# Two products with 64 weight columns in place of one with 128, in the search for each node's last edge

## The chip, the cores and the metric

The kernel runs on one core of a Trainium2 chip. The metric is the device time of one execution in microseconds, measured without the profiler. The program is one launch: two layers of a graph network (a normalisation, a graph convolution, an attention and a feed-forward part each) over 6250 nodes and 100000 edges, 256 features per node, float32.

## The reference

Only the first part of each layer matters here. The second layer's convolution takes for every node the features of the last edge that names it; which edge that is does not depend on the features, so the kernel finds it early, while the first layer's convolution runs.

```python
def _L0_gnn_ref(x, W, edge_index):
    src, dst = (edge_index[0], edge_index[1])
    h = x @ W
    deg = jax.ops.segment_sum(jnp.ones_like(dst, dtype=h.dtype), dst, num_segments=N)
    deg_inv_sqrt = jnp.where(deg > 0, jax.lax.rsqrt(jnp.maximum(deg, 1)), 0.0)
    norm = deg_inv_sqrt[src] * deg_inv_sqrt[dst]
    msgs = h[src] * norm[:, None]
    out = jax.ops.segment_sum(msgs, dst, num_segments=N)
    return out

def _L1_gnn_ref(x, edge_index, W, b):
    dst, src = (edge_index[0], edge_index[1])
    agg = jnp.zeros_like(x).at[dst].set(x[src])     # the last edge wins
    h = jnp.concatenate((x, agg), axis=-1)
    return h @ W.T + b

edge_index = jnp.stack([src, dst])
xn = _layernorm(x, axis=-1)
x = x + _L0_gnn_ref(xn, L0_gnn_W, edge_index) + _L0_mix_ref(...)[0]
x = x + _L0_ffn_ref(...)[0]
xn = _layernorm(x, axis=-1)
x = x + _L1_gnn_ref(xn, edge_index, L1_gnn_W, L1_gnn_b) + _L1_mix_ref(...)[0]
x = x + _L1_ffn_ref(...)[0]
```

## The kernel before

The program is a row of stages. The change touches one of them, `gather_stage` (names that begin with `gcn_` in the profile), which does the first layer's convolution, most of its attention, and the search for last edges.

The edges lie sorted by target in 784 tiles of 128 (padded). Four tiles make a group (GE = 4), so there are G = 196 groups, and two groups make a pair (PT = 8 tiles, 98 pairs). Per group POOL (GpSimd) issues four indirect gathers (L945; 782 in all, as the last group is short) that fetch 128 rows of `h_table` each into one of eight buffers `msg`; DVE builds one-hot matrices `hot` from the targets (`targets`, L1028); TensorE sums the messages by target, `acc = hot.T @ msg`, four float32 products of 128x128 weights and 256 columns (`sum_up`, L1152; each float32 product runs as two, so the profile has eight per group); DVE adds the sums to X (`add_up`, L1037).

Per pair the kernel also looks for the last edges. A source number is split into a low part (0 to 127) and a high part (0 to 48). DVE makes `lo_hot` (128 lanes, 128 low parts, 8 tiles, bf16, L1020) and `hi_eq` (49 high parts, L1023); ACT multiplies the latter with a power of two that grows with the lane, which gives `hi_hot` (`place`, L874). For each of the 8 tiles TensorE makes one product, `see` (L1159): weights `lo_hot[:, :, c]`, 128 rows and 128 columns, and moving operand `hi_hot[:, :, c]`, 49 columns. The tile is the last index of both, so two neighbouring columns of either operand lie 8 bf16 numbers (16 bytes) apart. The eight results lie side by side in one PSUM bank `seen`; the exponent of a sum names the highest lane, which is the last edge of the tile. ACT copies the bank (`keep_seen`, L879), and DVE merges the copy into what was seen so far by two predicated copies (`last_edges`, L1045 and L1047).

The order on each engine is written out by hand: the engines run through loops over eight groups, and the semaphores couple them. TensorE's queue for a pair is: sum of the even group, sum of the odd group, `see`, with the attention's products between (keys and values in the first loop, L1179 to L1184; the attention's output in the second, L1190 and L1191; nothing in the third). DVE's queue per group is: one-hots for the group four ahead (`sources`, `targets`), `add_up`, `last_edges`. So a merge that waits for `see` holds back the one-hots of the next group. POOL may run four groups ahead of TensorE: before group g it waits until group g-4 is summed (`after(pool, summed, g - NG + 1)`, NG = 4).

Two other products are of use for comparison. In the stage ahead `count_in` (L644, `front_deg`) makes products of 64 weight columns, bf16, with 98 moving columns; its operands' neighbouring columns lie 2 numbers (4 bytes) apart. In the last stage L2796 (`sel_ranks`) has 128 weight columns and 50 moving columns, bf16, also 4 bytes apart.

Of the kernel before, what the change touches and what calls it, by code (L numbers as in the profile page):

```python
# [24 lines left out]
P = 128  # L25
# [3 lines left out]
T = -(-N_NODES // P)  # L29
# [29 lines left out]
def after(eng, sem, n):  # L59

    if isinstance(n, int) and n <= 0:
        return
    eng.wait_ge(sem, n)
# [184 lines left out]
class Kernel:  # L248
# [456 lines left out]
    def gather_stage(self):  # L705

        nc, io = self.nc, self.io
# [5 lines left out]
        NS = 4  # L713
        NP = 2
# [3 lines left out]
        with ExitStack() as ctx:  # L718
# [3 lines left out]
            lo_hot = [s.sb(f"lo_hot{i}", [P, P, PT], BF16) for i in range(NS // 2)]  # L722
            hi_eq = [s.sb(f"hi_eq{i}", [P, T, PT], BF16) for i in range(2)]
            hi_hot = [s.sb(f"hi_hot{i}", [P, T, PT], BF16) for i in range(NS // 2)]
# [60 lines left out]
            seen = s.banks("seen", NP, PT * T)  # L785
# [66 lines left out]
            with nc.Block() as block:  # L852
# [287 lines left out]
                def _(pe):  # L1140
# [14 lines left out]
                    def see(h, k):  # L1155
                        after(pe, hi_ready, h + 1)
                        after(pe, lasts_kept, 2 * (h - NP + 1))
                        for c in range(PT):
                            last = nc.tensor.matmul(seen[k % NP][:, c * T:(c + 1) * T], lo_hot[k % NS][:, :, c], hi_hot[k % NS][:, :, c], start=True, stop=True)  # L1159
                        last.then_inc(seen_ready, 1)  # L1160

                    def groups(q, n):
                        for b in range(n):
                            sum_up(NB * q + b, b, q)
                            if b % 2 == 1:
                                see(NB // 2 * q + b // 2, b // 2)
# [26 lines left out]
                    for g in range(CHUNKED * NB):  # L1193
                        b, q = g % NB, g // NB
                        sum_up(g, b, q)
                        if b % 2 == 1:
                            see(g // 2, b // 2)
                        if g < NC:
                            key_chunk(g)
# [5 lines left out]
                    with pe.Fori(CHUNKED, ATT) as q:  # L1205
                        for b in range(NB):
                            n = NK * (q - CHUNKED) + sum(x < b for x in SLOTS) + 2
                            if b in SLOTS:
                                keys_and_values(n, SLOTS.index(b) % 2, P)
                            sum_up(NB * q + b, b, q)  # L1210
                            if b % 2 == 1:
                                see(NB // 2 * q + b // 2, b // 2)
                            if b in SLOTS:
                                context(n, P)
# [5 lines left out]
                    for b in range(KB):  # L1220
                        last = nc.tensor.matmul(side[:, b * D:(b + 1) * D], qc[:, b * P:(b + 1) * P], w_out, start=True, stop=True)
# [1693 lines left out]
```

## Time and profile before

| | us |
|---|---|
| median of three runs | 2759.92 (2756.18 to 2763.06) |
| span of the profiled execution | 2735.8 |
| median less span: what lies around it | 24.1 |
| gather stage, first gather issued to last one ended | 137.9 to 1280.2 |
| TensorE busy over the whole span | 2240.2 (82%) |
| POOL busy over the whole span | 1616.4 (59%) |
| DVE busy over the whole span | 1457.9 (53%) |
| the products of L1159, 784 of them, in the page's groups by form | 47.8 + 44.6 |

The span is the time from the first to the last instruction of one profiled execution. The profile gives no total for that execution beside its span; the median of the unprofiled runs is 24.1 us (0.9%) longer, which is launch and completion around it. The columns "busy" are sums over instructions; PE is TensorE's matmul side, PEld its weight loads. In a timeline, several instructions of one kind that follow each other are merged to one row with their count.

### The profile page before, as it was taken

How to read it: one execution, taken by the hardware profiler on the slowest of the kernel's cores; microseconds unless marked ns; L12 is line 12 of the kernel's file. 1: busy time of each engine (PE TensorE's matmuls, PEld its weight loads, DVE VectorE, ACT ScalarE, POOL GpSimd, SP SyncE). 2: the span in 40 equal slices, each digit the busy share in tenths (PEclk: the TensorE clock that was granted, in tenths of full speed). 3: DMA queues.
4: the chain of work that ended last, by engine and by line, in shares of the span. 5: the costliest groups of instructions: out<-in, count | busy, mean ns of one | idle time of the engine just before them, and what ended most of it. 6: DMA issues, size and time to landing. Idle time of an engine off the chain costs nothing. (4 is left out here: it accounts for less than half of the span.)

```text
span 2735.8 us, 47046 instructions
## 1 busy us (share of the span) xinstructions
PE 2240.2 (82%) x12461; PEld 1829.5 (67%) x12462; DVE 1457.9 (53%) x4032; ACT 826.7 (30%) x2317; POOL 1616.4 (59%) x2089
## 2 busy tenths in 40 slices
PE   7876767767666766655889999989998999996898
PEld 5644555555554544444869999967767888885798
DVE  9754433434444454435842223259987777777211
ACT  2511221221111111111623333335553333332333
POOL 5676666666666666764036555447857666661232
PEclk9987787878877886676589999999999999997999
DMA  4233332322333333333323334323221111111121
GB/s 159 98 99 87 88 92 86 90 86 86 91 90 87 91 91 92 92 90 85 118 77 106 106 123 138 104 78 101 88 68 55 44 46 42 44 46 62 30 37 29
DMA packets 139022, 227.27 MB, mean 83 GB/s; under 512 B 26923, under 2 KB 99456, under 8 KB 138946
## 3 DMA queue, kind: packets, MB, share of 16 engines
q0 software_dynamic: 56240, 142.70, 18.8%
q1 hardware_dynamic: 81186, 82.10, 9.0%
q10 hardware_dynamic: 1520, 1.58, 0.2%
q8 instruction: 34, 0.56, 0.1%
q14 instruction: 42, 0.34, 0.0%
HBM read 174.97 MB, written 51.30 MB: 83 GB/s over the span
## 5 line engine op out<-in xcount | busy, mean ns | idle before, releaser
L945 POOL DMA_INDIRECT all_XN<-h_table,l_srcI x782 | 780.3, 998 | 367.3 <-issue 219.1
L1152 PE MATMUL gcn_acc<-all_XN,gcn_hot 128*128 128x256 f32 x796 | 257.6, 475 | 110.9 <-DVE all_X L1037 54.4
L1152 PE MATMUL gcn_acc<-all_XN 128*128 128x256 f32 x768 | 248.1, 478 | 110.9 <-DVE all_X L1037 59.5
L1152 PEld LDWEIGHTS gcn_acc<-all_XN,gcn_hot 128*128 128x128 f32 x796 | 179.1, 236 | 171.6 <-DVE all_X L1037 76.6
L1152 PEld LDWEIGHTS gcn_acc<-all_XN 128*128 128x128 f32 x768 | 175.2, 239 | 164.6 <-DVE all_X L1037 69.5
L879 ACT COPY gcn_seen_sb<-gcn_seen 128x392 f32<-128x392 f32 x98 | 47.6, 485 | 576.2 <-remote 454.8
L1848 ACT ACTIVATE moe_hidden<-moe_hid_ps,moe_b 128x128 f32<-128x128 f32 x420 | 131.5, 364 | 281.5 <-PE moe_hid_ps L1929 250.0
L1929 PEld LDWEIGHTS moe_hid_ps<-moe_xst,held_held 128*128 128x128 f32 x1680 | 204.2, 193 | 12.0 <-issue 7.4
L1037 DVE SCALAR_TENSOR_TENSOR all_X<-gcn_acc,all_XN,all_X 128x256 f32 x392 | 170.6, 475 | 74.7 <-remote 59.2
L1929 PE MATMUL moe_hid_ps<-moe_xst,held_held 128*128 128x128 f32 x1680 | 207.5, 277 | 1.9 <-DVE moe_xst L1869 1.9
L1045 DVE COPY_PREDICATED gcn_last_seen<-gcn_seen_sb,gcn_seen 128x392 f32<-128x392 int32 x98 | 57.7, 589 | 277.6 <-ACT gcn_seen_sb L879 190.1
L1936 PE MATMUL moe_y_ps<-held_held,moe_hidden 128*128 128x256 f32 x840 | 198.9, 380 | 0.0
L2539 PE MATMUL att_f_ps<-held_held 128*128 128x256 f32 x784 | 191.0, 388 | 7.5 <-ACT held_held L2406 7.5
L2529 PE MATMUL att_hid_ps<-att_xpt,held_held 128*128 128x128 f32 x1568 | 184.2, 276 | 0.0
L2529 PEld LDWEIGHTS att_hid_ps<-att_xpt,held_held 128*128 128x128 f32 x1568 | 180.3, 193 | 0.1
L2539 PEld LDWEIGHTS att_f_ps<-held_held 128*128 128x128 f32 x784 | 141.7, 190 | 43.5 <-ACT held_held L2406 23.5
L1936 PEld LDWEIGHTS moe_y_ps<-held_held,moe_hidden 128*128 128x128 f32 x840 | 151.0, 190 | 16.9 <-issue 0.2
L1763 POOL DMA_INDIRECT moe_ring<-rows_table,moe_row x108 | 105.9, 981 | 84.0 <-POOL moe_row L1761 68.1
L1869 DVE COPY moe_xst<-moe_turned 128x256 f32<-128x256 f32 x106 | 45.0, 425 | 151.7 <-PE moe_turned L1909 125.8
L2060 POOL DMA_INDIRECT held_held<-slots_out,all_slot x98 | 99.6, 1016 | 36.0 <-issue 23.4
L1184 PE MATMUL gcn_tab<-all_XN 128*128 128x129 f32 (+1 forms) x98 | 27.2, 367 | 112.2 <-ACT all_XN L891 75.7
L2406 ACT ACTIVATE held_held<-att_hid_ps,early_b 128x128 f32<-128x128 f32 x392 | 111.4, 368 | 17.6 <-PE att_hid_ps L2529 17.6
(433 smaller groups left out, 4596.7 us busy)
## 6 DMA issues: line engine op xcount, KB each, us to landing
held_held<-in_e_w SPq DMA_DIRECT2D x32, 512.0 KB
slots_out<-moe_y SPq DMA_DIRECT2D x105, 128.0 KB
all_XN<-h_table,l_srcI POOLq DMA_INDIRECT x782
all_X<-in_x SPq DMA_DIRECT2D x7, 896.0 KB, 11.2
rows_table<-all_XN SPq DMA_DIRECT2D x7, 896.0 KB, 4.2
z_table<-held_held SPq DMA_DIRECT2D x49, 128.0 KB
x_table<-all_XN SPq DMA_DIRECT2D x49, 128.0 KB, 1.7
out<-all_X SPq DMA_DIRECT2D x49, 128.0 KB, 1.7
```

Source lines behind the costliest of these rows:

```text
L945: nc.gpsimd.indirect_dma_start(msg[b][:, c, :], None, self.h_table, bass.IndirectOffsetOnAxis(self.srcI[:, GE * g + c:GE * g + c + 1], 0)) ...
L1037: nc.vector.scalar_tensor_tensor(x, acc[b % NA][:, :], scale[:, k, ds(g, 1)], x, ALU.mult, ALU.add).then_inc(added, 1)
L1045: nc.vector.copy_predicated(last_seen[:, :], seen_sb[k % 2][:, :], seen[k % NP][:, :]).then_inc(lasts_kept, 1)
L1152: last = nc.tensor.matmul(acc[b % NA][:, :], hot[b % NH][:, c, :], msg[b][:, c, :], start=(c == 0), stop=(c == n - 1))
L1763: nc.gpsimd.indirect_dma_start(ring[:, k * D:k * D + D], None, self.rows_table, bass.IndirectOffsetOnAxis(row_1[k][:, :], 0)).then_inc(lan ...
L1848: last = nc.scalar.activation(hidden[:, 2 * k + f, :], hid_ps[k][:, f, :], ACT.Relu, bias=b1[:, c:c + 1])
L1929: last = nc.tensor.matmul(hid_ps[k][:, f, :], w1[p][:, q, c:c + P], xst[:, q, :], start=(q == 0), stop=(q == KB - 1))
L1936: last = nc.tensor.matmul(y_ps[:, :], hidden[:, f, :], w2[p][:, f, :], start=(f == 0), stop=(f == FB0 - 1))
L2060: nc.gpsimd.indirect_dma_start(ys[t % 2][:, c, :], None, self.slots_out, bass.IndirectOffsetOnAxis(self.slot[:, t, c:c + 1], 0)).then_inc( ...
L2406: last = nc.scalar.activation(hidden[:, c, :], hid_ps[k][:, f, :], ACT.Relu, bias=b1[:, c:c + 1])
L2529: last = nc.tensor.matmul(hid_ps[k][:, f, :], W1[:, b, c:c + P], xpt[:, b, :], start=(b == 0), stop=(b == KB - 1))
L2539: last = nc.tensor.matmul(f_ps[:, :], hidden[:, f, :], W2[:, f, :], start=(f == 0), stop=(f == FB1 - 1))
```

## The change

Each product of `see` becomes two. The first has the weight columns 0 to 63 and writes the lanes 0 to 63 of `seen`; the second has the columns 64 to 127 and writes the lanes 64 to 127. Both stream the same 49 moving columns. The 64 is the number of weight columns; all 128 rows are still used, and what is computed is the same. The semaphore is still raised by the last product alone. Per pair there are 16 products and 16 weight loads where there were 8 and 8; over the program 784 more of each.

```diff
@@ -1156,7 +1156,8 @@
                         after(pe, hi_ready, h + 1)
                         after(pe, lasts_kept, 2 * (h - NP + 1))
                         for c in range(PT):
-                            last = nc.tensor.matmul(seen[k % NP][:, c * T:(c + 1) * T], lo_hot[k % NS][:, :, c], hi_hot[k % NS][:, :, c], start=True, stop=True)
+                            for half in (slice(0, P // 2), slice(P // 2, P)):
+                                last = nc.tensor.matmul(seen[k % NP][half, c * T:(c + 1) * T], lo_hot[k % NS][:, half, c], hi_hot[k % NS][:, :, c], start=True, stop=True)
                         last.then_inc(seen_ready, 1)
```

On TensorE, in the body of the second loop (with the attention's output), the queue before reads as follows; the numbers behind a name are left out, x8 counts products, and L63 is the code of a wait.

```order
240 L1152 MATMUL gcn_acc<-all_XN,gcn_hot 128x256 x4
241 L63 ISA x2
242 L1159 MATMUL gcn_seen<-gcn_hi_hot,gcn_lo_hot 128x49 x8
243 L63 REGISTER_ALU x2
244 L1190 MATMUL gcn_side<-l_M,all_XN 128x256 x2
245 L1191 MATMUL gcn_side<-l_W,all_ones 128x256
```

And of the kernel with the change, in the same place (its lines behind L1159 are one higher):

```order
240 L1152 MATMUL gcn_acc<-all_XN,gcn_hot 128x256 x4
241 L63 ISA x2
242 L1160 MATMUL gcn_seen<-gcn_hi_hot,gcn_lo_hot 64x49 x16
243 L63 REGISTER_ALU x2
244 L1191 MATMUL gcn_side<-l_M,all_XN 128x256 x2
245 L1192 MATMUL gcn_side<-l_W,all_ones 128x256
```

Nothing has moved; the eight products with 128 output lanes have become sixteen with 64, between the same neighbours. The other engines' instructions are the same.

## Rows read from the trace of the kernel before

**Rows 1.** Windows of the whole gather stage, of its first loop and of its third
```profile
core 0: us, PE busy (x) PEld busy (x) DVE busy (x) ACT busy (x) POOL busy (x), PEclk, DMA share, GB/s
137.90:1280.20 1142.30, 774.37 (x3078) 573.02 (x3079) 504.38 (x1070) 206.44 (x488) 780.28 (x782) 0.78 0.31 90
400.00:500.00 100.00, 73.64 (x311) 57.57 (x312) 38.83 (x80) 21.79 (x63) 66.20 (x67) 0.78 0.30 88
1100.00:1200.00 100.00, 61.75 (x210) 43.46 (x211) 43.86 (x92) 15.28 (x30) 70.50 (x70) 0.71 0.32 92
```

**Rows 2.** Waits in the stage: who waited for whom, us in total, times, longest
```profile
ACT gcn_seen_sb L879 <- remote: 454.8, 55, 25.9
DVE gcn_last_seen L1045 <- ACT gcn_seen_sb L879: 190.1, 29, 21.3
...
POOL all_XN L945 <- remote: 107.5, 45, 4.1
ACT gcn_seen_sb L879 <- PE gcn_seen L1159: 98.9, 27, 7.2
...
POOL all_XN L945 <- PE gcn_acc L1152: 34.5, 19, 7.5
```

**Rows 3.** Timeline near 440 us (idle before, releaser); last a window as in rows 1
```profile
437.58 1.99 PE L1152 MATMUL gcn_acc<-all_XN,gcn_hot 128*128 128x256 f32 x8
...
439.20 0.91 PEld L1159 LDWEIGHTS gcn_seen<-gcn_hi_hot,gcn_lo_hot 128*128 128x128 bf16 x8
...
439.41 0.92 PE L1159 MATMUL gcn_seen<-gcn_hi_hot,gcn_lo_hot 128*128 128x49 bf16 x8
440.48 0.94 POOL L945 DMA_INDIRECT all_XN<-h_table,l_srcI  x1 [0.30 <-issue]
...
444.23 0.80 PE L1184 MATMUL gcn_tab<-all_XN 128*128 128x129 f32 x2 [3.90 <-ACT all_XN L891]
...
447.50 0.49 ACT L879 COPY gcn_seen_sb<-gcn_seen 128x392 f32<-128x392 f32 x1 [2.80 <-remote]
447.56 0.94 POOL L945 DMA_INDIRECT all_XN<-h_table,l_srcI  x1 [2.38 <-remote]
...
439.20:440.40 1.20, 1.13 (x10) 0.84 (x8) 0.00 (x0) 0.00 (x0) 0.95 (x1) 1.00 0.36 109
```

**Rows 4.** Durations of L1159: ns min/median/max, first and last start, form
```profile
L1159 PEld LDWEIGHTS gcn_seen<-gcn_hi_hot,gcn_lo_hot x400: 140/146/175, 157.1 to 1276.6; 128*128 128x128 bf16 x134
L1159 PE MATMUL gcn_seen<-gcn_hi_hot,gcn_lo_hot x400: 246/274/287, 157.3 to 1276.7; 128*128 128x49 bf16 x134
```

**Rows 5.** Timeline near 1047 us, where the same products stand apart
```profile
1046.03 0.15 PEld L1159 LDWEIGHTS gcn_seen<-gcn_hi_hot,gcn_lo_hot 128*128 128x128 bf16 x1 [1.58 <-issue]
1047.43 0.14 PEld L1159 LDWEIGHTS gcn_seen<-gcn_hi_hot,gcn_lo_hot 128*128 128x128 bf16 x1 [1.26 <-issue]
...
1046.73 0.25 PE L1159 MATMUL gcn_seen<-gcn_hi_hot,gcn_lo_hot 128*128 128x49 bf16 x1 [1.86 <-issue]
1048.13 0.25 PE L1159 MATMUL gcn_seen<-gcn_hi_hot,gcn_lo_hot 128*128 128x49 bf16 x1 [1.15 <-issue]
```

**Rows 6.** L2796, one burst of ten; its window (busy, granted clock); its durations
```profile
2534.87 0.57 PE L2796 MATMUL sel_ranks<-sel_node_part,all_XT 128*128 128x50 bf16 x10 [6.17 <-ACT sel_node_part L2659]
...
2534.80:2540.40 5.60, 2.80 (x50) 0.50 0.00 0
...
L2796 PEld LDWEIGHTS sel_ranks<-sel_node_part,all_XT x49: 102/119/123, 2534.8 to 2540.2; 128*128 128x128 bf16 x49
L2796 PE MATMUL sel_ranks<-sel_node_part,all_XT x49: 200/217/220, 2534.9 to 2540.2; 128*128 128x50 bf16 x49
```

**Rows 7.** Durations of L644 (64 weight columns) and of its neighbour L667
```profile
L644 PEld LDWEIGHTS front_deg<-all_XN x784: 107/109/172, 8.3 to 101.5; 128*64 128x64 bf16 x196
L644 PE MATMUL front_deg<-all_XN x784: 205/208/290, 8.3 to 101.6; 128*64 128x98 bf16 x196
...
L667 PE MATMUL front_h_ps<-l_W,all_XT x196: 379/379/763, 45.5 to 132.3; 128*128 128x256 f32 x196
```

**Rows 8.** Timeline near 61 us, around sixteen products of L644; last its window
```profile
60.13 0.69 DVE L560 TENSOR_TENSOR all_XN<-front_dst_lo,all_XN 128x1024 bf16<-128x1024 bf16 x1
60.18 1.03 PE L667 MATMUL front_h_ps<-l_W,all_XT 128*128 128x256 f32 x4
...
61.14 0.78 PEld L644 LDWEIGHTS front_deg<-all_XN 128*64 128x64 bf16 x16 [0.33 <-DVE all_XN L560]
61.14 0.92 PE L644 MATMUL front_deg<-all_XN 128*64 128x98 bf16 x16
...
61.99 0.44 PE L653 MATMUL front_turned<-all_ident,all_XN 128*128 128x128 f32 x2
...
61.10:62.10 1.00, 1.00 (x18) 0.89 (x18) 1.00 (x2) 0.69 (x2) 0.96 (x2) 1.00 0.00 0
```

**Rows 9.** Timeline near 905 us: `see` behind a slow sum, then a fast one
```profile
901.96 3.41 PE L1152 MATMUL gcn_acc<-all_XN 128*128 128x256 f32 x8 [3.27 <-DVE all_X L1037]
...
905.20 0.92 PE L1159 MATMUL gcn_seen<-all_XN 128*128 128x49 bf16 x8
...
905.94 1.93 PE L1152 MATMUL gcn_acc<-all_XN,gcn_hot 128*128 128x256 f32 x8
```

## The prediction

> **What bounds the kernel now.** I read the busy shares first, then cut out the stage that holds `see`, then its waits, and last the timeline. The stage takes 1142 of 2736 us, and nobody is full in it: TensorE is busy 774 us (68%), POOL 780 (68%), DVE 504 [rows 1]. The pace is POOL's. A gather takes 0.94 us and the next follows 0.30 later [rows 3], so a group of four takes 4.96 us and the 782 gathers 782 x 1.24 = 970 us. The remaining 172 us of the stage are gathers that came late. POOL waited 107.5 us in 45 waits that the profile calls remote and 34.5 us in 19 waits for the sum L1152 [rows 2]: 64 waits, 142 us, in which the sum four groups back was not yet reported. So TensorE's time costs something where its queue is late, and nothing else.
>
> How late it can be is seen near 440 us: the sum ended at 439.57 (437.58 + 1.99) and `see` at 440.33, but POOL went on at 447.56 and ACT copied `seen` at 447.50 [rows 3]. Between them TensorE had nothing of them to do. I don't know what holds these reports back; it is a part of the 142 us that is not TensorE's work, and I keep it apart. ACT's and DVE's large waits, 454.8 and 190.1 us, are of this kind, with 98.9 us that ACT waits for `see` itself [rows 2].
>
> **The change part by part.** Removed: 8 products and 8 loads per pair. Added: 16 and 16. No engine but TensorE has other work. A `see` now takes 0.92 us [rows 3, 9]. Its last product lasts 0.27 [rows 4], so the products start (0.92 - 0.27)/7 = 93 ns apart.
>
> What are the 93 ns? L2796 has the same shape, 128 weight columns and 50 moving ones, and its ten products take 0.57 us, (0.57 - 0.22)/9 = 39 ns apart, at half clock (0.50, that is 1.2 GHz) [rows 6]. In L1159 the pace is 93 ns at full clock (1.00, 2.4 GHz) [rows 3]. The difference between the two in the code is the distance of neighbouring columns, 16 bytes against 4. And it shows on the moving side: where the loads of L1159 stand 0.70 us ahead of their products, with the weights long in place, a product still takes 0.25 us [rows 5], while a product with twice the columns, 98, takes 0.208 [rows 7] and one with 50 columns 0.217 at half clock [rows 6]. If 98 columns close together cost 98/2.4 = 41 ns (L644 ran at 1.00 [rows 8]), the fixed part is 0.167 and the 49 distant ones cost some 80 ns, nearly the whole pace. The halved products stream the same 49 columns. So I take 93 ns for each half, and 15 x 0.093 + 0.27 = 1.67 us for the sixteen: **+0.75 us** per `see`.
>
> The bounds of this pace: below, L644 with its 64 weight columns makes sixteen products in 0.92 us [rows 8], (0.92 - 0.21)/15 = 47 ns apart, which gives 15 x 0.047 + 0.25 = 0.96 us, +0.04. Below that, with L2796's 39 ns or less, and if two halves ran side by side at some 25 ns apiece, 15 x 0.025 + 0.25 = 0.63, -0.29. Above, if 64 weight columns are read one by one as slowly as the moving ones (93/49 = 1.9 ns a column), a load lasts 122 ns and is the pace: 15 x 0.122 + 0.27 = 2.10, +1.18. I stay at 93, the measured pace of the same operands.
>
> The second term is the passage between the two shapes. L667's last product starts at 60.18 + 1.03 - 0.38 = 60.83; at its pace of 0.216 ((1.03 - 0.38)/3) the next would start at 61.05, and L644 starts at 61.14: 0.09 late. The DVE instruction named there had ended at 60.82 [rows 8], so it was not that. Leaving: L644's last product starts at 61.14 + 0.92 - 0.21 = 61.85, 0.047 later would be 61.90, and L653 starts at 61.99: 0.09 late. In `see` before there is no such loss on leaving: last start 905.20 + 0.92 - 0.27 = 905.85, next product 905.94, one pace of 0.09 [rows 9]. So **+0.18 us** per `see`; the bounds are 0 and 0.2. The Trainium skill, "TensorEngine Tiling (Array Packing)", section "Tiling Modes", says that changing the tiling mode drains the TensorE, while changing the tile within a mode does not; the trace agrees with the first (0.09 us each way), and by the second the change between lower and upper half adds nothing, which I assume too.
>
> Together 0.75 + 0.18 = 0.93 us per `see`, 98 x 0.93 = 91 us more TensorE work in a stage where TensorE is idle 1142 - 774 = 368 us. What lands? In steady pace nothing: in the third loop TensorE has 61.75 us of work in 100 us [rows 1], about 7.1 us for a pair (100/70 x 8 = 11.4 us for its eight gathers, times 0.62) against the 9.9 us that POOL needs; 8.0 still fits. In the first loop (73.6 in 100, a pair per 11.9 us) 8.8 becomes 9.7: just. What hides the addition is thus POOL's pace, and it is gone where POOL waits. The sum that POOL waits for has, in TensorE's queue and since the last free moment, about one `see` ahead of it (there is one for two sums). The 19 waits for L1152 grow by 0.93 us each in full; of the 45 remote ones I count two thirds, 30, since part of them ends on the unexplained delay and not on work. 49 x 0.93 = **+45 us**. There is a second path of the same length: ACT's copy comes 0.93 later, DVE's merge behind it, and behind the merge in DVE's queue the one-hots for a later sum [rows 2]; it runs into the same waits of POOL and is not counted twice.
>
> Against its own execution: 2735.8 + 45 = 2781 for the span, and 24.1 around it gives 2805, which is the median 2759.9 + 45. No difference under 0.3% (8 us) can be told from none here.
>
> **The rivals.**
> (a) The weight load becomes the pace: 0.122 us a product, 1.18 + 0.18 = 1.36 us per `see`, 49 x 1.36 = 67 us, 2827. For it: L1159's loads last 146 ns against 119 in L2796 at half clock [rows 4, 6], so they too are slowed by the distance. Against: L644's loads with 64 columns last 109 [rows 7], less than those of 128. By the Trainium skill, "TensorE: Matmul & The Clock Gate", section "Weight-path perf modes", the fast weight load applies only to 128 weights that are not fp32, and the tiling page's list of incompatibilities has column tiling exclude it; the halves would then lose it. That is the mechanism under which 0.122 would hold, and no row of before has 64 columns at this distance.
> (b) Everything is hidden: the waits end on the delayed reports alone, as at 447.56 [rows 3], and POOL's pace covers the rest. Then 0 to 8 us, about 2763. For it: TensorE itself had been idle for 3.90 us when it went on at 444.23 [rows 3], so its queue was not the cause there. Against: 19 waits are put down to L1152.
> (c) Faster: the two halves have different weights and different output lanes and run side by side, so that `see` takes 0.63 + 0.18 = 0.81 us or less, and with no loss at the passages 0.63. Price: 64 x -0.29 = -19 us, 2741. It decides from a pace below 44 ns per product (15 x 0.044 + 0.25 = 0.92). For it: 25 to 39 ns is possible for this engine [rows 6]; against: the moving columns' 80 ns, and the passages. The Trainium skill, "TensorE: Matmul & The Clock Gate", section "Part 3: Packing small matmuls", has small products on different column groups run concurrently; no row of before shows two such products together.
> (d) The late reports become more with the number of products (784 more on 3078 in the stage, +25%): the 142 us of waiting grow by a quarter, 36 us, on top of 45: about 2841.
>
> **How the numbers follow.** Forecast 2805: chance 0.45. (a) 0.17, (b) 0.18, (c) 0.13, (d) 0.07. Range: the low end leaves out most of (c), 2750; the high end takes in (a) and (d) together with all 64 waits at 1.36 + 36 us, 2760 + 87 + 36 = 2883, 2885. The likeliest case alone: 49 waits give 45, 19 waits 18 and all 64 with 0.93 60, so 2778 to 2820. Faster by over 0.3%: (c), 0.13, and 0.01 of (b). Within 0.3%: 0.15 of (b) and 0.03 of the forecast's lower edge, 0.18. Slower: the rest of the forecast 0.42, (a) 0.17, (d) 0.07 and 0.02 of (b), 0.68.
>
> **What would show it.** In the profile of the changed kernel a run of sixteen products should last 1.6 to 1.7 us (0.96 would be the lower bound, 2.1 rival (a), 0.6 to 0.8 rival (c)); a product alone still 0.25. The loads should be at or below 146 ns; 190 would be (a). The first product behind a sum should start 0.31 after the sum's last instead of 0.22. TensorE's work in the stage should be up by about 80 us and the granted clock by a few hundredths. The stage should be longer by 45 us, all in POOL's waits; gathers keep 0.94 + 0.30. Other stages should keep their times. I would be wrong if the run of sixteen is below 0.92 us, or if it is 1.6 us and the stage no longer.

## The result, and the profile after

| | before | after |
|---|---|---|
| median of six runs | 2758.05 us (2746.84 to 2763.06) | 2775.75 us (2771.28 to 2786.76) |
| ratio | | 1.0074, 95% interval 1.005 to 1.0097 |
| span of the profiled execution | 2735.8 us | 2776.9 us |

The change costs 18 to 20 us where 45 were forecast (2805). The direction and the range are right, the size is not. The two spans differ by 41 us. That is no measure of the change: the run in which the after profile was taken needed 2778.77 us, so only 1.9 us lie around a span. The profile of before came from an execution quicker than each of its timed runs. I had read the 24.1 us between its span and the median as launch and completion; most of it is scatter from one execution to the next.

Each of the 18 kernels below is compared only with runs of before from its own session, as before itself differs between sessions: its medians are 2743.17 us beside kernels 1 to 4, 2756.72 beside 5 to 8, 2756.79 beside 9 to 12, 2758.48 beside 13 to 16, and 2607.61 (23 runs, 2604.02 to 2612.08) beside 17 and 18. Kernels 5 to 8 and 17 and 18 ran on the same chip, so the 150 us are not a difference between two chips.

Windows of the kernel after, as in [rows 1] (columns as there):

```profile
137.90:1280.20 1142.30, 826.66 (x3733) 588.94 (x3734) 485.66 (x1030) 201.72 (x478) 750.24 (x755) 0.78 0.30 87
400.00:500.00 100.00, 77.60 (x363) 57.83 (x364) 43.37 (x89) 22.99 (x68) 64.64 (x65) 0.81 0.29 84
1100.00:1200.00 100.00, 59.99 (x262) 43.80 (x263) 38.39 (x80) 13.91 (x27) 67.66 (x69) 0.69 0.31 90
```

TensorE has 52 us more busy time in the same 1142 us, and POOL has got through 755 gathers instead of 782. Before and after, cut where the stage of each ends:

```profile
130.00:1290.00 1160.00, 782.07 (x3112) 578.86 (x3110) 512.24 (x1089) 209.97 (x496) 781.42 (x784) 0.78 0.31 90
1290.00:2735.00 1445.00, 1351.46 (x8280) 1165.13 (x8280) 830.71 (x2699) 562.64 (x1694) 756.76 (x1148) 0.94 0.25 74
```

```profile
130.00:1330.00 1200.00, 858.20 (x3894) 611.77 (x3892) 513.07 (x1089) 210.20 (x496) 780.31 (x784) 0.78 0.30 87
1330.00:2776.00 1446.00, 1351.41 (x8280) 1165.55 (x8280) 830.38 (x2698) 562.68 (x1694) 757.52 (x1148) 0.94 0.25 74
```

Behind the stage nothing has changed (1351.46 and 1351.41 us of TensorE work, 1445 and 1446 us). Inside it the instructions of the other engines are the same in number and cost, TensorE has 782 products more and 76 us more of busy time (41 of them in `see` itself, 92 to 133 us; the rest is spread over its other products).

`see` in the timeline of after near 441 us, against [rows 3, 9]:

```profile
437.86 3.26 PE L1152 MATMUL gcn_acc<-all_XN 128*128 128x256 f32 x8
439.99 0.95 POOL L945 DMA_INDIRECT all_XN<-h_table,l_srcI  x1 [1.49 <-remote]
...
441.05 1.18 PE L1160 MATMUL gcn_seen<-all_XN 128*64 128x49 bf16 x16
...
442.15 1.13 PE L1180 MATMUL gcn_side<-l_W,all_XN 128*128 128x256 f32 x4
...
449.88 1.16 PE L1160 MATMUL gcn_seen<-gcn_hi_hot,gcn_lo_hot 128*64 128x49 bf16 x13
451.49 0.36 PE L1160 MATMUL gcn_seen<-gcn_hi_hot,gcn_lo_hot 128*64 128x49 bf16 x3 [0.45 <-issue]
...
437.80:441.00 3.20, 3.20 (x10) 2.38 (x8) 0.88 (x2) 0.00 (x1) 1.65 (x2) 0.56 0.29 82
```

The sixteen products take 1.18 us where 1.67 were forecast. The sum at 437.86 takes 3.26 us instead of 1.99 [rows 3], but that is the clock and not the change: the granted clock around it is 0.56 (last line), and before has such sums too, 3.41 us at 901.96 [rows 9]. Something else is to be seen. The run of sixteen at 449.88 is broken once: the last three stand 0.45 us apart from the others with "issue" as the reason, so TensorE waited for nothing that the profile shows. By single records, such steps are 0.70 us from one instruction to the next, in bursts. I count in the stage the steps of 0.6 us or more, start to start, between two loads or products that stand next to each other in TensorE's records with no wait or other sequencer instruction at or between them: 50 before, with 40 us in them, and 143 after, with 115 us. I call them stalls. (The 62 and the "119 to 164" that an expectation below names come from a wider count of the same steps.) Half of them in after, 73, stand in the third loop.

The durations of the half products, against [rows 4]:

```profile
L1160 PEld LDWEIGHTS gcn_seen<-gcn_hi_hot,gcn_lo_hot x800: 192/217/226, 157.2 to 1317.7; 128*64 128x64 bf16 x160
L1160 PE MATMUL gcn_seen<-gcn_hi_hot,gcn_lo_hot x800: 246/300/348, 157.2 to 1317.8; 128*64 128x49 bf16 x160
```

The waits of after, against [rows 2]; the last line is one of before that is not shown there:

```profile
ACT gcn_seen_sb L879 <- remote: 515.7, 56, 22.8
...
POOL all_XN L945 <- remote: 128.1, 66, 4.0
ACT gcn_seen_sb L879 <- PE gcn_seen L1160: 122.9, 32, 7.3
PEld gcn_seen L1160 <- issue: 107.8, 165, 2.6
...
POOL all_XN L945 <- PE gcn_acc L1152: 64.4, 26, 15.3
...
PEld gcn_seen L1159 <- issue: 30.4, 45, 6.6
```

POOL's waits have grown from 142.0 to 192.5 us, by somewhat more than the 40 us between the two stages; as these are two single executions, and before's was a quick one, only about half of that can be the change. TensorE's own row is larger: 107.8 us of "issue" ahead of the loads of `see`, where before has 30.4.

The late reports themselves can be measured, as the trace also holds the time of each semaphore update. I set each update that reports a sum beside the last sum that had ended by then (20 of 193 updates of before are missing in the trace, and a lag longer than the distance of two sums is taken too short). In before the update comes 2.0 us after the sum's end in the median, 3.3 in the mean, and 110 of 173 come over 1 us late. Nearly all updates by DVE and ACT in this stage come 7 to 12 ns after their instructions' ends. So of these three engines TensorE alone reports late. In after they are no later: median 2.4 us, mean 3.1, 119 of 185 over 1 us.

### The profile page after: what moved, and what is told of

Same layout as the page of the kernel before. It is cut to its first block and busy times, and to the rows that moved or that the text cites. A ratio compares the mean times of both kernels' runs of the same rounds, so it can differ in the third digit from the quotient of the medians.

```text
span 2776.9 us, 48614 instructions
## 1 busy us (share of the span) xinstructions
PE 2317.1 (83%) x13245; PEld 1863.4 (67%) x13246; DVE 1458.3 (53%) x4032; ACT 827.2 (30%) x2317; POOL 1616.1 (58%) x2089
## 5 line engine op out<-in xcount | busy, mean ns | idle before, releaser
L1152 PE MATMUL gcn_acc<-all_XN,gcn_hot 128*128 128x256 f32 x796 | 273.1, 496 | 92.3 <-DVE all_X L1037 49.7
L1152 PE MATMUL gcn_acc<-all_XN 128*128 128x256 f32 x768 | 236.1, 457 | 67.1 <-DMA all_XN<-h_table,l_srcI 31.9
L1152 PEld LDWEIGHTS gcn_acc<-all_XN,gcn_hot 128*128 128x128 f32 x796 | 188.0, 247 | 153.5 <-issue 65.0
L1152 PEld LDWEIGHTS gcn_acc<-all_XN 128*128 128x128 f32 x768 | 167.0, 228 | 115.0 <-issue 60.5
L1901 DVE TENSOR_TENSOR moe_y<-moe_y_ps,moe_b 128x256 f32<-128x256 f32 x105 | 44.6, 425 | 133.0 <-PE moe_y_ps L1937 100.1
```

What stands on the lines that cost most here:

```text
L1152: last = nc.tensor.matmul(acc[b % NA][:, :], hot[b % NH][:, c, :], msg[b][:, c, :], start=(c == 0), stop=(c == n - 1))
```

## The experiments

The expectations were written before each kernel ran. The ratio is that to before in the same session, with its 95% interval; "work" is TensorE's busy time in 137.9 to 1280.2 us (774.37 before, 826.66 after). Where the cost of a kernel is given in us or ns, it is the ratio's. A slower kernel gets less far in this window, so I also give the busy time of the whole stage, against the 782 us of before (after: +76).

**1. Lower halves first.** All eight lower halves, then all eight upper.

```diff
-for c in range(PT):
-    for half in (slice(0, P // 2), slice(P // 2, P)):
+for half in (slice(0, P // 2), slice(P // 2, P)):
+    for c in range(PT):
```

> The sixteen half products of a pair in another order: the eight lower halves first, then the eight upper ones. The profile of the change shows the two halves of a tile starting 1 to 7 ns apart and the next two 120 ns later, with loads of 217 ns. Theory A (the load of 64 weight columns lying 16 bytes apart takes 120 ns and sets the pace; two halves overlap because they use different columns of the array): in this order neighbours use the same columns, the products start 120 ns apart, a run of sixteen lasts 15 x 0.12 + 0.30 = 2.1 us, TensorE has 98 x 1.38 = 135 us more work than before, and if 0.37 of it lands as in the change (20 of 52 us) the time is 50 us above before, about 2808. Theory B (the number of products and the two passages between shapes cost the time, not the loads): same number, same passages, so the same time as the change, about 2776.

Measured: 2765.27 us, ratio 1.0082 (1.0058 to 1.0106). Windows and loads:

```profile
137.90:1280.20 1142.30, 872.74 (x3799) 644.19 (x3799) 495.53 (x1051) 203.85 (x482) 768.31 (x769) 0.79 0.31 89
```

```profile
L1160 PEld LDWEIGHTS gcn_seen<-gcn_hi_hot,gcn_lo_hot x800: 192/217/217, 157.3 to 1299.5; 128*64 128x64 bf16 x160
```

Products of the same half start 118 to 120 ns apart. The run of sixteen lasts 1.70 us and not the 2.1 expected, as in its middle upper halves already start between the last lower ones.

```profile
441.59 1.69 PE L1160 MATMUL gcn_seen<-all_XN 128*64 128x49 bf16 x16
```

In after, the two halves of a tile start 1 to 7 ns apart and the next tile's follow 118 ns later, by single records. So two effects that I had as rivals are both there: a half load lasts 217 ns and sets a pace of 120, and two different halves go side by side. TensorE has 98 us more work than before here, nearly twice the change's 52 (whole stage: +111 against +76), and the time is that of the change. That speaks against work as the cause.

**2. Whole products twice.** `for _ in range(2):` around the loop of before, sixteen products of 128 columns.

> Before, with every whole product (128 weight columns) made twice, so sixteen products per pair, no change of shape. Theory A: they start 93 ns apart, a run of sixteen lasts 15 x 0.093 + 0.27 = 1.67 us, the see of a pair costs 0.74 us more than before, 98 x 0.74 = 73 us of TensorE work, of which 0.37 lands: +27 us, about 2785. Theory B with the passages as the cause (no passages here): no slower than before by more than 5 us, 2758 to 2763. Theory B with the number of products as the cause: 2776, like the change. My prediction's share (a half of TensorE's added work lands): +36 us, 2794.

Measured: 2763.7 us, 1.0077 (1.0053 to 1.0101), products 93 to 95 ns apart, 81 us more work (whole stage: +94):

```profile
137.90:1280.20 1142.30, 854.88 (x3794) 642.96 (x3795) 496.26 (x1048) 203.94 (x482) 762.14 (x769) 0.79 0.31 89
```

No other shape, no passage, another amount of work, the same number of products, and the same loss.

**3 and 4. Columns close together.** The one-hots are laid out in pairs of tiles, so that neighbouring columns stand 4 bytes apart and not 16; with whole products (3) and with halves (4).

```diff
-lo_hot = [s.sb(f"lo_hot{i}", [P, P, PT], BF16) ...]
+lo_hot = [s.sb(f"lo_hot{i}", [P, PT // 2, P, 2], BF16) ...]
-hi_hot = [s.sb(f"hi_hot{i}", [P, T, PT], BF16) ...]
+hi_hot = [s.sb(f"hi_hot{i}", [P, PT // 2, T, 2], BF16) ...]
...
-... lo_hot[k % NS][:, :, c], hi_hot[k % NS][:, :, c] ...
+... lo_hot[k % NS][:, c // 2, :, c % 2], hi_hot[k % NS][:, c // 2, :, c % 2] ...
```

> Before, with the low and the high one-hots laid out in pairs of tiles, so that neighbouring columns of both operands lie 4 bytes apart instead of 16; whole products of 128 weight columns. Theory A (distance of the columns sets the pace): the eight products start about 25 to 30 ns apart, a see takes 0.45 us instead of 0.92, 98 x 0.47 = 46 us less TensorE work; at the share of 0.37 that is 17 us, about 2741. If only TensorE's waits count and a see that gets shorter frees nothing: 2758. Theory B (number of products): no change, 2758. DVE's two operations that build the one-hots should keep 0.69 and 0.35 us.

> The same close layout, with the halves of the change. Theory A: a load of 64 columns 4 bytes apart takes 27 ns (109 in the profile with the fixed part), so sixteen products in about 0.6 us plus two passages of 0.1 us each, a see about as long as before's 0.92 or a little below: 2750 to 2762. Against the close layout with whole products it should be 5 to 20 us slower, by the passages and the number. Theory B (number and passages cost it all): as slow against its own base (whole products, close) as the change is against before, about +18 us.

Measured: whole 2748.43 us, 1.0015 (0.9997 to 1.0033); halves 2766.92, 1.0085 (1.0059 to 1.0111). Whole, then halves:

```profile
L1159 PEld LDWEIGHTS gcn_seen<-gcn_hi_hot,gcn_lo_hot x400: 96/98/152, 157.3 to 1291.5; 128*128 128x128 bf16 x134
L1159 PE MATMUL gcn_seen<-gcn_hi_hot,gcn_lo_hot x400: 183/188/248, 157.5 to 1291.6; 128*128 128x49 bf16 x134
```

```profile
L1160 PEld LDWEIGHTS gcn_seen<-gcn_hi_hot,gcn_lo_hot x800: 106/115/159, 157.1 to 1302.0; 128*64 128x64 bf16 x160
...
137.90:1280.20 1142.30, 756.19 (x3771) 530.56 (x3772) 492.68 (x1047) 204.19 (x482) 761.69 (x764) 0.76 0.30 88
```

The whole products now start 27 ns apart at full clock, 42 at half, where they had needed 93 at either. So the distance of the columns was the price, as the forecast had it; both operands were moved at once, so these two kernels don't tell which of them costs it. But the 35 us of work that this saves (whole stage: 32) bring nothing; and halving costs 0.7% here although sixteen close halves take 0.45 us, half of before's 0.92, and TensorE has no more work than the kernel before (18 us less in the window, 5 less in the whole stage).

**5. One product instead of eight.** A single product of all 392 moving columns with the first tile's weights; the search of the other seven tiles is left out. 686 products and loads fewer.

```diff
-for c in range(PT):
-    last = nc.tensor.matmul(seen[...][:, c * T:(c + 1) * T], lo_hot[...][:, :, c], hi_hot[...][:, :, c], ...)
+last = nc.tensor.matmul(seen[...], lo_hot[...][:, :, 0], hi_hot[...], ...)
```

> See made with one product instead of eight: the weights of the first tile alone and all 8 x 49 = 392 moving columns (so seven of eight results have the wrong weights; the searched edges are not the right ones). The moving columns still lie 16 bytes apart, so they should stream in 392 x 1.67 = 0.65 us, about the work of before's eight (0.75), with 7 products and 7 loads fewer per pair, 686 of each over the program. Theory A (TensorE's busy time is what costs): -0.1 us per see, time within 4 us of before. Theory B (each product and load costs, whatever it does: the four kernels with 784 more were 20 to 24 us slower, 28 ns each): 686 x 0.028 = 19 us less than before. If the cost sets in only above a number of instructions: no change.

Measured: 2737.49 us, 0.992 (0.9894 to 0.9946), with unchanged work (2 us less in the whole stage): 22 us for 686, 32 ns for each product with its load. The one product tells something else too:

```profile
439.20 0.85 PE L1159 MATMUL gcn_seen<-gcn_hi_hot,gcn_lo_hot 128*128 128x392 bf16 x1
```

It takes 0.85 us for 392 moving columns and one load. Less the 0.167 us that the forecast worked out as fixed, that is 1.7 ns a column or 85 ns for 49, near the forecast's 80. By this estimate the distance on the moving side alone makes up nearly the whole pace of 93.

**6, 7 and 8. More instructions, little work.** 8 or 24 further products of one moving column per `see` (6, 7); sixteen further `sem_inc` on TensorE, which are no products (8).

```diff
+for _ in range(24):
+    nc.tensor.matmul(seen[k % NP][:, 0:1], small_ones[:, 0:P], small_ones[:, 0:1], start=True, stop=True)
```

> Before, with eight further products ahead of each see, of one moving column and 128 constant bf16 weights that lie 4 bytes or less apart: about 25 ns each, 0.2 us of TensorE work per see (20 us over the program), 784 products and loads more, no change of shape. Theory A (work, of which a third lands): +7 us or less. Theory B (number): +20 to +24 us, like the four kernels with 784 more.

> The same with 24 further small products per see: 2352 more of each over the program, about 0.6 us of work per see (59 us). Theory A: +22 us at most. Theory B, if each costs 28 ns: +66 us; more if it is a supply that runs short.

> Before, with 16 increments of an unused semaphore on TensorE's queue ahead of each see, so 1568 more instructions, as many as the 784 loads and 784 products of the change, but none of them uses the array. Theory B1 (the supply of TensorE's instructions, of whatever kind, runs short; the profile has stalls of 0.70 us between instructions that wait for nothing, 62 before and 119 to 164 with sixteen products): +20 to +24 us and stalls above 110. Theory B2 (only products and loads cost): what the increments take themselves, some 50 ns each if nothing hides them, 0.8 us per see, of which a third lands: +26 us; so the time alone doesn't tell, but the stalls would stay near 62.

Measured: 2772.61 us, 1.0052 (1.0033 to 1.0071); 2835.36, 1.0282 (1.025 to 1.0313); 2772.09, 1.0042 (1.0022 to 1.0062). The last has no product more than before. Its waits:

```profile
PEld gcn_seen L1161 <- issue: 74.9, 65, 9.3
...
POOL all_XN L945 <- PE gcn_acc L1152: 50.5, 27, 7.0
```

The first line is not stalls. The increments stand 151 ns apart in the records, so sixteen take 2.4 us of TensorE's sequencer, and `see` comes late where the sums ahead do not cover that (its first product starts over 0.7 us behind the sum's last in 18 of 94 cases, and in none of 96 before). By the count above this kernel has 35 stalls, fewer than before's 50. Of the two theories B1 asked for stalls above 110, and that is refuted; B2's sign, as few stalls as before, came out, with +0.42% (12 us) where it had 26. So 8 shows a price for the sequencer's time and not one for the number of instructions, and the argument from the number rests on the products (1, 2, 4 to 7).

**9, 10 and 11. POOL runs further ahead.** `NG = 6` in place of 4, before and changed, and `NG = 8` before: POOL waits for an older sum, with the same eight `msg` buffers.

```diff
-        NG = 4
+        NG = 6
```

> Before, with POOL allowed to run six groups ahead of TensorE's sums instead of four (NG = 6). Theory C (what TensorE's stalls cost comes in by POOL's waits for a sum four groups back, 142 us of them in before): most of these waits go, as they are 1 to 4 us long and two more groups give 10 us: 60 to 120 us less, 2640 to 2700. If TensorE's stalls bound the stage by themselves, through the one-hots and the sums' own order: 0 to 20 us less.

> The change, with NG = 6. Theory C: the same time as before with NG = 6, within 6 us, since the added stalls no longer reach POOL. Otherwise: 18 to 25 us above before with NG = 6, as with NG = 4.

> Before with NG = 8, as far as the eight message buffers allow. Theory C: as NG = 6 or up to 20 us better, POOL's waits near zero, the stage at 782 x 1.25 = 978 us plus its start. Otherwise as NG = 6.

Measured: 2758.27 us, 1.0011 (0.9991 to 1.0032); 2778.35, 1.0083 (1.0056 to 1.011); 2765.99, 1.0036 (1.0013 to 1.006). POOL's waits stay (119.5 and 37.9 us with six in the unchanged kernel), and so does the loss by the change. If single sums that are a microsecond late were what POOL waits for, two groups more of run-ahead, 10 us, would have covered them. So theory C is refuted and its alternative came out. The plain reading, which no run isolates, is that with reports this late TensorE's side of the stage is on the whole no faster than the gathers come, and that POOL's waits only pass this on.

**12 to 14. The change in one loop at a time:** in the third (12; 192 products more, as its edit leaves the last two of the 26 pairs whole), in the unrolled part and the first (13; 320), in the second (14; 256). `see` gets an argument for it.

> The change only in the last 26 of 98 pairs (third loop and what follows it), 208 more products and loads. In that loop TensorE has no attention products and the fewest instructions per group. Theory B1 with a supply that costs the same everywhere: 208/784 of 20 us, +5 us. If the number matters only where the queue is dense (first two loops, with attention): 0.

> The search's products are halved only for the 40 pairs of the unrolled part and of the first loop (320 products more on TensorE). Theory (the number of instructions on TensorE costs time where its queue is also full of the attention's products): the whole change costs +0.74%, and in the profile after the first loop's share of the loss was about 19 us of the 31 seen in the gathers, so +0.35 to +0.5%. Rival 1 (the cost is the same for each product wherever it stands): 320/784 of 0.74%, +0.30%. Rival 2 (no part of it is lost before POOL's waits of the second loop are made longer): 0 here.

> The search's products are halved only for the 32 pairs of the second loop (256 products more). Theory: what is left of the 0.74% once the first loop has its share, +0.25 to +0.4%, and together with the kernel halved in the first loop alone it makes 0.7 to 0.8%. Rival 1 (the same for each product): +0.24%. Rival 2 (all of it falls in the first loop): 0.

Measured: 2757.37 us, 0.9992 (0.9974 to 1.0011); 2763.72, 1.0014 (0.9991 to 1.0037); 2761.79, 1.0013 (0.9995 to 1.0031). None can be told from nothing. The theory's +0.35% and more for the first loop was too high; that the three together fall short of 0.74% is suggestive, but three intervals of 0.2% each don't settle it.

**15 and 16. Where an instruction is dear.** The 24 small products per `see` in the third loop alone (576 more), and in the unrolled part and the first loop alone (960).

> 24 further products of one moving column in front of each search of the third loop alone, which has no attention products (24 pairs, 576 products and loads more, nearly as many as the whole change adds). Theory (what counts is instructions in a dense queue): nothing here, within 0.3% of before, since TensorE is idle 38% of that loop; the 0.70-us stalls may well be more in number. Rival (each added product costs some 28 ns wherever it stands, because the instruction supply itself is what bounds): 576 x 28 ns = 16 us, +0.6%.

> 24 further products of one moving column in front of each search of the unrolled part and the first loop (40 pairs, 960 products and loads more). With 24 everywhere (2352 more) the time was 2.8% longer, 33 ns apiece. Theory (dense queue): two thirds or more of the 2.8%, +1.6 to +2.2%, some 50 to 60 us and 50 to 60 ns apiece, with the first loop's gathers late by that much. Rival (the same for each): 960/2352 of 2.8%, +1.1%, 32 us.

Measured: 2762.82 us, 1.003 (1.0008 to 1.0053), and 2816.23, 1.021 (1.0181 to 1.0238): 14 ns apiece (4 to 25 by the interval) and 60. First the waits of the third-loop kernel, then those of the first-loop one:

```profile
PEld gcn_seen L1160 <- issue: 78.1, 83, 2.7
...
POOL all_XN L945 <- PE gcn_acc L1152: 31.9, 17, 6.3
```

```profile
POOL all_XN L945 <- PE gcn_acc L1152: 118.7, 38, 15.0
POOL all_XN L945 <- remote: 112.1, 46, 4.1
```

And the 24 small products of the first-loop kernel in its timeline:

```profile
404.71 0.82 PE L1160 MATMUL gcn_seen<-all_ones 128*128 128x1 bf16 x24
```

They start 29 ns apart, (0.82 - 0.16)/23, and take some 0.7 us of TensorE; they cost 58 us in 40 pairs, 1.4 us a pair. So an added product costs more than its work where the queue is dense, and half its work's length where it is not; the number alone is not the rule either. Nor do the visible stalls measure it: the third-loop kernel has 162 and 133 us in them for +0.3%, the first-loop one 55 and 46 us for +2.1%, and the unchanged kernel with `NG = 6` (9) has 104 and 99 us for +0.1%.

A rival stands in the windows of the first loop, before's and then kernel 16's, each with the part of the sums (L1152) alone behind it:

```profile
137.90:607.10 469.20, 325.87 (x1350) 242.36 (x1350) 206.21 (x435) 95.33 (x258) 319.07 (x320) 0.80 0.31 91
137.90:607.10 469.20, 182.84 (x616) 131.91 (x616) 0.80 0.31 91
```

```profile
136.80:671.00 534.20, 415.02 (x2263) 309.42 (x2264) 205.28 (x435) 95.91 (x259) 314.54 (x321) 0.71 0.28 80
136.80:671.00 534.20, 216.18 (x616) 154.25 (x616) 0.71 0.28 80
```

The loop is 65 us longer, and the granted clock in it is 0.71 instead of 0.80; kernel 7 has 0.72 there. The same 616 products of the sums take 33 us more. So a part of the 60 ns, and of the 33 of kernel 7, is clock and not the price of an instruction; how large a part, no run separates. The change itself has no such term: over the stage the clock is 0.78 in before and after.

Of the waits, what grew in kernel 16 is POOL's for the sum, 118.7 us against 34.5 [rows 2].

**17 and 18. Both dense loops, and a session without late reports.** Halves in the unrolled part, the first and the second loop (17; 576 more), 24 small products in the second loop (18; 768 more).

> The search's products are halved for the 72 pairs of the unrolled part and of the first and second loops, and left whole in the third loop (576 products more). If the parts simply add, this is what the two kernels halved in one of these loops showed together, +0.27% (+0.14 and +0.13, each with +-0.2), and the change as a whole would owe +0.47% to the third loop, which alone showed nothing. If what one loop leaves behind (a merge or a copy that runs late) is paid in the next, it is nearer the whole change: +0.6 to +0.8%. I hold the second for somewhat likelier.

> 24 further products of one moving column in front of each search of the second loop alone (32 pairs, 768 products and loads more). First loop alone: +2.1% for 960, third loop alone +0.3% for 576, everywhere +2.8% for 2352. If the places add, the second loop has 0.4% (11 us, 14 ns apiece). The rule that a dense queue pays (TensorE has attention products here too, fewer than in the first loop) would have it between the two others per product: 15 to 60 ns, +0.4 to +1.6%.

Measured: 2607.41 us, 0.9998 (0.9989 to 1.0006), and 2605.51, 0.9991 (0.9981 to 1.0001), with before at 2607.61. Neither expectation has been tested as it was meant, since the kernel before was itself 150 us shorter; but what the profile shows is worth more. The waits of 17 in the gather stage:

```profile
ACT gcn_seen_sb L879 <- PE gcn_seen L1160: 496.7, 95, 11.1
DVE gcn_last_seen L1045 <- ACT gcn_seen_sb L879: 266.8, 54, 7.6
POOL all_XN L945 <- issue: 230.6, 757, 0.3
PE gcn_acc L1152 <- DMA all_XN<-h_table,l_srcI: 200.0, 118, 3.5
PEld gcn_seen L1160 <- issue: 29.8, 81, 0.7
...
POOL all_XN L945 <- PE gcn_acc L1152: 7.3, 24, 0.3
```

Of POOL's 192.5 us of waiting after (142.0 before), 7.3 are left, the longest 0.3 us. No wait in the stage is remote any more, and 3 stalls are left where the kernel before had 50 and the changed one 143. The reports of the sums, measured as above, come 14 ns after the sum's end, and none of 195 comes over 1 us late; in 18 it is the same. Its gathers:

```profile
L945 POOL DMA_INDIRECT all_XN<-h_table,l_srcI x782: 942/946/1956, 138.0 to 1150.0; - x196
```

The last starts at 1150.0 us, 128 earlier than in the profile of before and 168 earlier than in that after (1318.5). `see` is as long as in the changed kernel:

```profile
443.80 1.19 PE L1160 MATMUL gcn_seen<-gcn_hi_hot,gcn_lo_hot 128*64 128x49 bf16 x16
444.91 0.49 PE L1185 MATMUL gcn_tab<-all_XN 128*128 128x129 f32 x2
...
447.26 1.99 PE L1152 MATMUL gcn_acc<-all_XN,gcn_hot 128*128 128x256 f32 x8 [0.58 <-DMA all_XN<-h_table,l_srcI]
```

Now TensorE waits for the gathers, 118 times, and the longer `see` comes out of these waits: with 73% of the change's products in halves the time is that of before (interval -0.11 to +0.06%). The kernel before was not profiled beside 17 and 18; that its reports came in time there too is inferred from its 2607.61 us.

## Why the prediction was wrong

- **What bounds the kernel: right only without the late reports.** I had POOL's pace with waits on top. In 17 it is POOL's pace: the stage takes 1013 us with 7.3 us of waits. (My floor of 970 was 43 too low: I took the common 0.94 us for all 782 gathers, 735 us, and with the longer ones they take 776 there.) In the other sessions a longer run-ahead of POOL brought nothing (9, 11), so there its waits are a sign of the lateness and not what limits the stage. That the other stages keep their times, and that the profiled stage grows in POOL's waits, came out.
- **The pace of a half product: mis-sized.** I took 93 ns for each and 1.67 us for sixteen, and set rivals (a) and (c) on either side. Both hold. A load of 64 distant columns lasts 217 ns against 146 [rows 4] and sets the pace I had worked out for (a), 118 to 120 ns against 122; and two halves run side by side, (c), so it is paid eight times and not sixteen. The Trainium skill, "TensorE: Matmul & The Clock Gate", section "Part 3: Packing small matmuls", has products on different column groups run concurrently; the trace agrees (starts 1 to 7 ns apart). The Trainium skill, same page, section "Weight-path perf modes", keeps the fast weight load to 128 weights; the trace agrees (217 against 146 ns), and the close layout shows the same in small (115 against 98).
- **The passages: nearly right.** From the sum's last product to the first half 0.31 us (0.22 before), as forecast; from the last half to the next product 0.23 instead of 0.09, +0.14 where +0.09 was forecast. Start to start a `see` with its passages is 1.42 us against 0.96: **+0.47 instead of +0.93**, 98 x 0.47 = 46 us of TensorE's time and not 91. This term alone explains the number that was missed: 49 x 0.47 is 23 us and 49 x 0.93 is 45. The sign I had named, some 80 us more TensorE work, was met with 76, but only 41 of them are in `see`; the granted clock stayed at 0.78 where I had it rise.
- **What lands: the step that failed.** I had TensorE's added work land in 49 of POOL's 64 waits. With the measured 0.47 this gives 23 us, close to the measured 18 to 20, but that is luck. It doesn't hold as the cause: with 111 and 94 us more work in the stage the loss is the same (1, 2); with no more work than before it is the same (4); 32 us less work gains nothing (3); two groups more of run-ahead neither save time nor take the loss away (9, 10). What went with the time in those sessions is how many products TensorE takes: 26 to 29 ns for a product and its load (after, 1, 2, 4), 32 for one taken away (5), 18 and 33 for small ones (6, 7), 60 in the first loop and 14 in the third (16, 15). The 33 and the 60 hold a part that is the clock's, and no mechanism is shown for the rest.
- **The late reports: I set apart what mattered.** I wrote that what holds the reports back is not TensorE's work and kept it as a constant; rival (d) alone let it grow with the number of products, with a chance of 0.07 and 36 us, on top of the 45. The measured 20 us stand where (d)'s 36 would be with nothing under them, but (d) is not shown either: the reports of the sums are no later after the change (mean 3.1 us against 3.3). 17 and 18 show that this delay is no property of the kernel: without it POOL hardly waits, and neither the halves nor 768 small products cost anything measurable. There rival (b)'s result holds, everything is hidden, and by its second reason alone: POOL's pace covers it.

What stays open: what slows TensorE's instructions to 0.70 us a step and the reports with them in some sessions and not in another. It is not the gathers: they take 0.94 to 0.95 us each in both kinds, and the packets of their queue 18.8% of 2735.8 us in before and 19.8% of 2604.6 in 17, about 515 us in both. That it is tied to how TensorE is supplied with instructions is not shown, and 8 speaks against it; open is also how more products cost time there when the lag of the reports does not grow, and how much of the 60 ns of the first loop is the clock's. The halving of all pairs was not run in the undisturbed session; for the 26 last pairs, which are whole there, the only measurement is 12's 0.9992 (24 of them, in a session with late reports).

## What to carry to other kernels

Before a change is priced by an engine's busy time, look whether the waits for that engine are put down to "remote": then its reports may be late, saved work may bring nothing (3), and more products can cost time even without more work (4; here some 30 ns for a product and its load). Run the kernel before beside the changed one each time, since a delay of this kind may be gone in the next session, here with 150 us and with the effect of three quarters of the change. For bf16 one-hots, put a product's neighbouring columns close together, and if the weight columns are halved at all, let two different halves follow each other directly (1.18 us for sixteen, against 1.70 in the order of 1).

## What the runs showed of the hardware

- The distance of an operand's columns sets a product's pace: 49 moving and 128 weight columns take 93 to 95 ns with 16 bytes between columns, at either clock, and 27 ns (42 at half clock) with 4 bytes (before, 3). 392 moving columns at 16 bytes take 0.85 us (5).
- A weight load of 64 columns is slower than one of 128: 217 against 146 ns at 16 bytes, 115 against 98 at 4.
- Products on the two halves of the output lanes start 1 to 7 ns apart if they follow each other; in a row on one half they stand 118 to 120 ns apart. Going to halves costs 0.09 us and coming back 0.14 (after). A semaphore increment in TensorE's queue takes 151 ns to the next (8).
- In all sessions but the last, TensorE shows steps of 0.70 us between instructions in the gather stage, and its reports to other engines come late, those of the sums by 2.0 us in the median in before, while nearly all of DVE's and ACT's come within 12 ns; in the last session those of the sums come 14 ns after the sum's end (17, 18). The stage takes 1142 us before the change, and 1013 in the last session with most of the halves in. The difference between the two medians of the kernel before, 2757 and 2608 us, is 5.4%, more than anything this change does.
